# Two transformer layers on one core: the second layer's projections taken in pairs of tiles with split operands

## The reference

```python
xn = _layernorm(x, axis=-1)
x = x + attn0(xn) + ffn0(xn)      # ffn0: the two best of 8 experts for each token
xn = _layernorm(x, axis=-1)
# second attention: blocks of 64 tokens, 8 heads of 32
q = xn @ Wq + bq;  k = xn @ Wk + bk;  v = xn @ Wv + bv
probs = softmax(q @ k.T * 32 ** -0.5)          # within a block, so its rows sum to 1
attn = (probs @ v) @ Wo + bo
# second mixture: each of 8 experts takes the 512 tokens with its highest scores
scores = (xn @ Wg.T).T
x = x + attn + ffn1(xn, scores)
```

## Time and profile before

| | |
|---|---|
| median of 3 runs | 825.96 us (825.92 to 827.94) |
| the profiled execution | 833.11 us |
| its span, from the first to the last instruction | 831.3 us |
| busy share of the span | PE 93%, DVE 68%, POOL 54%, ACT 47% |
| mean granted PE clock | 0.973 of full speed |
| DMA | 114.92 MB, 138 GB/s over the span |

### The profile page before, as it was taken

How to read it: one execution, slowest core, us unless ns; L and a number is a source line. 1 busy time by engine, 2 the same in 40 slices (tenths; PEclk the granted TensorE clock), 3 DMA queues, 4 the chain that set the end, 5 groups by cost and what they waited for, 6 DMA issues and landing times.

```text
span 831.3 us, 20019 instructions
## 1 busy us (share of the span) xinstructions
PE 772.4 (93%) x6524; PEld 685.8 (82%) x6524; DVE 566.8 (68%) x1351; ACT 390.2 (47%) x936; POOL 448.6 (54%) x553
## 2 busy tenths in 40 slices
PE   6989989999999999999969999989889879999993
PEld 4867754899999999999959999867678668888883
DVE  5766776566666666667557777689999665677651
ACT  5343425444444444444415554536667564455430
POOL 3756666044445443569478888313358343666335
PEclk9999999999999999999989999969999998999997
DMA  8666632233343433344266666324547754665324
GB/s 268 229 192 234 219 110 77 74 111 121 117 125 110 121 110 122 108 144 144 80 193 200 198 196 194 108 46 112 115 100 168 201 180 140 139 140 141 65 26 50
DMA packets 140606, 114.92 MB, mean 138 GB/s; under 512 B 49890, under 2 KB 130786, under 8 KB 140516
## 3 DMA queue, kind: packets, MB, share of 16 engines
q1 hardware_dynamic: 127652, 87.94, 35.2%
q0 software_dynamic: 12288, 25.31, 13.3%
q10 hardware_dynamic: 576, 0.52, 0.2%
HBM read 68.77 MB, written 40.76 MB: 132 GB/s over the span
## 4 chain that ended last, share of the span: by engine, by line
PE 75%; DVE 9%; issue 7%; another core or an unknown queue 3%; ACT 3%; POOL 1%; DMA 0%; POOLq 0%; DVEq 0%; ACTq 0%
PE bank L838 15%; PE banks L856 12%; PE bank L1066 11%; PE bank L896 8%; PE banks L1082 4%; PE banks L766 3%; PE banks L777 3%; PE banks L712 2%; PE bank L976 2%; PE bank L825 2%; PE bank L905 2%; PE banks L905 2%; PE bank L959 2%; PE banks L911 1%
## 5 line engine op out<-in xcount | busy, mean ns | idle before, releaser
L838 PE MATMUL bank<-rw,rt 128*128 128x128 f32 x1136 | 138.6, 275 | 0.9 <-ACT rw L1170 0.6
L838 PEld LDWEIGHTS bank<-rw,rt 128*128 128x128 f32 x1136 | 132.5, 192 | 1.8 <-issue 1.3
L856 PE MATMUL banks<-r_split,rt_split 128*128 x852 | 118.7, 289 | 0.1
L1994 POOL TENSOR_TENSOR rw<-r,rw 128x128 f32<-128x128 f32 x64 | 41.3, 646 | 137.1 <-DMA rw<-in_sin_q 137.1
L856 PEld LDWEIGHTS banks<-r_split,rt_split 128*128 128x128 f32 x852 | 106.0, 190 | 0.3 <-issue 0.3
L1066 PE MATMUL bank<-r_split 128*128 128x512 f32 x384 | 91.5, 398 | 4.6 <-issue 4.5
L1982 POOL DMA_INDIRECT rows_by_expert<-rw,slots x64 | 66.5, 1039 | 46.7 <-DVE slots L1500 28.8
L1066 PEld LDWEIGHTS bank<-r_split 128*128 128x128 f32 x384 | 73.3, 193 | 20.2 <-issue 5.1
L1609 DVE TENSOR_TENSOR rt_split<-rw,rt_split 128x512 fp32r<-128x512 f32 x71 | 54.1, 763 | 49.4 <-ACT rt_split L1221 49.4
L1603 DVE TENSOR_TENSOR rw<-rw 128x512 f32<-128x512 f32 x71 | 53.5, 753 | 43.3 <-ACT rw L1215 43.2
L2100 POOL DMA_INDIRECT out_x<-r,idx x32 | 50.2, 1569 | 59.9 <-DVE r L1880 52.2
(11 more groups left out here) (255 smaller groups left out, 1646.7 us busy)
## 6 DMA issues: line engine op xcount, KB each, us to landing
rt<-in_w SPq DMA_DIRECT2D x24, 512.0 KB, 4.1
rw<-rows_by_expert SPq DMA_DIRECT2D x71, 128.0 KB
results_by_slot<-rw SPq DMA_DIRECT2D x71, 128.0 KB, 2.0
r<-in_w SPq DMA_DIRECT2D x16, 512.0 KB
rw<-in_x SPq DMA_DIRECT2D x16, 256.0 KB
rw<-in_sin_q SPq DMA_DIRECT2D x32, 128.0 KB
rw<-x_layer SPq DMA_DIRECT2D x32, 128.0 KB
rows_layer<-rw SPq DMA_DIRECT2D x32, 128.0 KB
```

Source lines behind the costliest of these rows:

```text
L838: last = pe.matmul(bank[1 + t % 2][:, k * P:(k + 1) * P], c_w1[:, t % 2, c, k * P:(k + 1) * P], c_xT[:, t % 2, c, :], start=c == 0, stop=c ...
L856: last = pe.matmul(bank[6 + t % 2][:, 0:D], h[:, t % XB, c, :], w[:, ds(e2, 1), o + c * D:o + (c + 1) * D], start=n == 0, stop=n == 3 * HC ...
```

## The change

- Stage D works in units of two tiles (NU = 16). PE transposes four 128x128 blocks of a unit into one bank (`transpose_unit`), ACT writes the high part (`high_xT`), DVE the low part (`low_xT`).
- Queries and keys of a unit: 4 output blocks of 256 columns, each 6 float32r matmuls (`queries_keys`, 24 in all). Values and scores together: 264 columns for each tile, 6 matmuls each (`values_scores`, 12 in all).
- The normalised tiles are written by ACT (`normal_unit`, Identity with scale and bias, as L1135 does in stage A) instead of DVE. ACT also moves the values and the scores out of PSUM (`keep_values_scores`).
- The bias of the values isn't added to them. As the softmax rows sum to 1, it goes through Wo: PE computes bv Wo once (`bias_of_values`), and DVE adds it to bo before stage D.
- POOL in stage D only gathers, up to eight tiles ahead in eight buffers, with a wait that the gather four tiles before has landed. SP stores x without bias (`x1_complete`), and loads and stores two tiles by one DMA. In stage E `add_x` first adds the bias to the loaded x and then the result, two POOL instructions a tile instead of one.
- The weights of the projections are split once in stage C: a copy on ACT at t = 20 and a subtraction and a small copy on DVE at t = 22.
- PE's and ACT's parts of stage D are loops of the engine as before, with two and four units a turn; before they held two tiles a turn.

```diff
+            def low_xT(u):
+                dve.wait_ge(aT_sb, NT + u + 1)
+                dve.tensor_tensor(d_lo[:, u % 2, :, :], bank[u % 2][:, :].rearrange("p (c n) -> p c n", c=DC),
+                                  d_hi[:, u % 2, :, :].bitcast(F32), ALU.subtract).then_inc(xlo_d, 1)
+            for u in range(NU + 1):          # DVE
+                if u < NU:
+                    combine(u, 0)
+                    combine(u, 1)
+                    moments_unit(u)
+                    scale_unit(u)
+                if u >= 1:
+                    low_xT(u - 1)
+            def transpose_unit(v):           # PE; 4 transposes into bank[v.k % 2]
+                pe.wait_ge(xn_r, NT + 2 * (v.u + 1))
+                if v.at_least(2):
+                    pe.wait_ge(xlo_d, v.u - 1)
+            def queries_keys(v):
+                pe.wait_ge(xlo_d, v.u + 1)
+                for b in range(2):
+                    if v.at_least(1):
+                        pe.wait_ge(qk1_sb, 4 * v.u + 2 * b - 2)
+                    for j in (2 * b, 2 * b + 1):
+                        for c in range(DC):
+                            for w, x in ((wq1_hi, d_hi), (wq1_hi, d_lo), (wq1_lo, d_hi)):
+                                last = pe.matmul(bank[2 + b][:, j % 2 * D:(j % 2 + 1) * D], w[:, c, j * P:(j + 1) * P],
+                                                 x[:, v.k % 2, c, :], start=k == 0, stop=k == 3 * DC - 1)
+            with pe.Fori(2, NU // 2) as m:
+                for k in range(2):
+                    transpose_unit(Unit(m, k, 2))
+                    project_before(Unit(m, k, 2))   # queries_keys, values_scores of the unit before
+            def step_d(v, more=True):        # ACT
+                if v.at_least(1) and more is not None:
+                    high_xT(v.back(1))
+                if more:
+                    root_unit(v)
+                    normal_unit(v)
+                if v.at_least(2):
+                    keep_queries_keys(v.back(2))
+                    keep_values_scores(v.back(2))
             def gather_y(t):                 # POOL
-                if t >= XB:
-                    pool.wait_ge(x1_r, t - XB + 1)
+                if t >= 2 * DB:
+                    pool.wait_ge(x1_r, t - 2 * DB + 1)
+                if t >= 4:
+                    pool.wait_ge(dy_in[t % 4], 32 * (t // 4))
-                pool.wait_ge(x1_r, t + 1)
-                if t >= 2:
-                    pool.wait_ge(sd.xb_out[t % 2], 16 * (t // 2))
-                pool.tensor_tensor(d_xb[:, t % 2, :], d_x[:, t % XB, :], bo1_s[:, :], ALU.add).then_inc(sd.xb, 1)
             def add_x(s):                    # POOL, stage E
+                pool.wait_ge(xbl[s.par], 16 * (s.half + 1))
+                pool.tensor_tensor(e_xb[:, s.par, :], e_xb[:, s.par, :], bo1_s[:, :], ALU.add).then_inc(bo1_r, 1)
+                pool.wait_ge(bo1_r, s.t + 1)
                 pool.wait_ge(y1_sb, s.t + 1)
-                pool.wait_ge(xbl[s.par], 16 * (s.half + 1))
                 pool.tensor_tensor(e_y[:, s.t % 4, :], e_y[:, s.t % 4, :], e_xb[:, s.par, :], ALU.add).then_inc(fin_r, 1)
```

More of the change, by code:

```diff
@@ L668, in _ @@
         def _(pe):
-            def transpose_x(z, s, xn, n=NT):
-                pe.wait_ge(z.xn, z.first + s.t + 1)
-                if s.at_least(1):
-                    pe.wait_ge(z.xT, z.first + s.t)
-                for c in range(DC):
-                    last = pe.transpose(bank[0][:, c * P:(c + 1) * P], xn[:, s.par, c * P:(c + 1) * P], ident[:, :])
-                last.then_inc(z.xT_ps, 1)
             pe.wait_ge(made, 2)
@@ L914, in _, with bias_of_values @@
-            for t in range(4):
-                step_d(Step(t // 2, t % 2))
-            with pe.Fori(2, NT // 2) as m:
-                for par in range(2):
-                    step_d(Step(m, par))
-            step_d(Step(NT // 2, 0))
+            def bias_of_values():
+                pe.wait_ge(wq1_r, 3)
+                pe.wait_ge(y_sb, ST0)
+                for c in range(DC):
+                    last = pe.matmul(bank[7][:, 0:D], bv1_b[:, c, :], wo1_s[:, c, :], start=c == 0, stop=c == DC - 1)
+                last.then_inc(bo1_ps, 1)
@@ new lines, in values_scores @@
+            def values_scores(v):
+                if v.at_least(1):
+                    pe.wait_ge(bo1_ps, 2)
+                if v.at_least(2):
+                    pe.wait_ge(sc_kept, v.u - 1)
+                par = v.k % 2
+                for i in range(2):
+                    k = 0
+                    for c in range(DC):
+                        for x, w in ((d_hi, wq1_hi), (d_lo, wq1_hi), (d_hi, wq1_lo)):
+                            last = pe.matmul(bank[4 + par * 2 + i][:, 0:D + E], x[:, par, c, i * P:(i + 1) * P],
+                                             w[:, c, 2 * D:3 * D + E], start=k == 0, stop=k == 3 * DC - 1)
+                            k += 1
+                last.then_inc(vs_ps, 1)
@@ new lines, in root_unit, with normal_unit @@
+            def root_unit(v):
+                act.wait_ge(mom_r, NT + 2 * (v.u + 1))
+                if v.at_least(2):
+                    act.wait_ge(rs_r, NT + v.u - 1)
+                act.activation(d_sd[:, v.k % 2, :], d_mv[:, v.k % 2, :, 1], ACT.Sqrt, bias=eps_c[:, :]).then_inc(std_r, 1)
+            def normal_unit(v):
+                act.wait_ge(nm_r, NPR + v.u + 1)
+                if v.at_least(2):
+                    act.wait_ge(xn1_out[v.k % 2], 16 * v.pair)
+                    act.wait_ge(aT_ps, NT + v.u - 1)
+                for i in range(2):
+                    act.activation(d_xn[:, v.k % 2, i, :], d_x[:, v.k, i, :], ACT.Identity,
+                                   bias=d_nm[:, v.k % 2, i:i + 1], scale=d_rs[:, v.k % 2, i:i + 1]).then_inc(xn_r, 1)
@@ new lines, in step_d @@
+            def step_d(v, more=True):
[4 more added lines that the diff above has]
+                    normal_unit(v)
+                if v.at_least(2):
+                    keep_queries_keys(v.back(2))
+                    keep_values_scores(v.back(2))
+            for k in range(DB):
+                step_d(Unit(0, k, DB))
+            with act.Fori(1, NU // DB) as m:
+                for k in range(DB):
+                    step_d(Unit(m, k, DB))
```

303 lines of the change are left out of this document (144 added, 159 removed).

## The result

The changed kernel takes 850.41 us (median), 1.030 times the kernel before on the same chip (interval 1.026 to 1.034): 24.5 us slower, where 7.6 us less were forecast and 835.7 was the worst case named. Two later comparisons, on other chips, gave 1.029 and 1.031. The profiled execution took 851.61 us, with a span of 849.9.

What follows compares the result with a forecast made beforehand. PE was taken to bound stage D before the change, POOL's gathers after it. Stage D's gain of 15.9 us, less 0.3 in stage C and 8.0 in stage E, gave 7.6 us less: 818.4 us, range 809 to 828.

Steps and rivals of the forecast that it cites:

- Stage D, POOL: Stage D: four gathers a unit make POOL the bound at 5.3 us, above PE's 4.87; stage gain 15.9 us.
- the three values for the pitch: Stage D, time from gather to gather on POOL: 1.37 us taken, ends 1.32 (never meeting DVE's additions) and 1.50 (always).
- PE, DVE, ACT: Stage D, work per two-tile unit: PE 4.87 us, DVE 4.8, ACT 4.8 to 4.9, none exceeding POOL.
- The ends: Stage D's end: last gather done 504.1, landed 508.0, then 14.15 us of work; stage E starts at 522.2.
- Stage C: Stage C, splitting the weights once on ACT and DVE: costs 0.3 us, bounds 0 and 2.
- Bias of the values: Before stage D, four PE instructions (0.9 us) and one DVE addition: hidden behind DVE's wait for the first gather, otherwise 1.3 us.
- Stage E: Stage E, POOL's second addition a tile: costs 8.0 us (search 1, threshold and ranks 1.8, one-hots 5.2), bounds 2 and 18.
- E swallowed nothing: Rival: stage E hides POOL's new addition under DVE's PSUM work, costing 2 us; kernel at 812.4 us; chance 0.20.
- Exclusion on gathers: Rival: DVE and POOL exclude each other, gather pitch 1.50, stage E costs 17.2; 9.7 us slower, 835.7; chance 0.13.
- The loop through four engines: Rival: stage D's dependency loop through DVE, ACT and PE takes 6.0 us a unit; 825.8 us, no change; chance 0.12.
- gathers that wait for `x1_r`: Stage D, named sign that the forecast is wrong: POOL's gathers wait for the combination of tiles.
- a unit over 5.8 us: Stage D, named sign that the forecast is wrong; a two-tile unit was expected at 5.3 to 5.7 us.

Runs made afterwards that it cites:

- e1: Changed kernel plus one 128x512 memset on POOL behind each tile's two gathers in stage D: 830.34 us, ratio 1.0047 to the kernel before.
- e3: Changed kernel with gathers of the first four tiles only, the other 28 reusing their rows (results differ): 806.14 us, ratio 0.978 to the kernel before.
- e7: Changed kernel plus a 128x16 memset on POOL behind each tile's two gathers, on the chip without stalls: 808.44 us, ratio 0.9991 to the kernel before.
- e16: Changed kernel with POOL's bias addition back in stage D, gathers three tiles ahead, one addition a tile in stage E: 835.95 us, ratio 1.0057.
- e5: Kernel before without POOL's bias addition in stage D (results differ), on the chip without stalls: 814.48 us, ratio 1.0070 to the kernel before.
- e18: Changed kernel unaltered, run again on the fifth chip: 858.57 us, ratio 1.0305 to the kernel before.
- e10: Kernel before, unaltered, run again on the third chip: 827.29 us, ratio 1.0001.
- e9: Changed kernel unaltered, run again on the third chip: 850.39 us, ratio 1.0293 to the kernel before.

## Where the prediction held and where it failed

- **Stage D, POOL: this step failed.** "A unit has 4 gathers ... 5.3 us a unit, more than PE's 4.87. POOL becomes the bound." The step gave a gather a price on POOL alone. I looked for what others do to a gather (DVE holding it, the DMA share going to 0.80) and never for what gathers do to others. POOL's addition stood in the sum as a cost that goes away; it was also the break that kept PE running. Its price for that was nothing, without a reason given. What the runs show in its place is a wait of 32.9 us at one copy of ACT alone, and a stage D that is 17.4 us longer instead of 15.9 shorter; with breaks (e1) or without most gathers (e3) the wait is gone.
- Its small terms: the pitch of bare gathers is (457.64 - 416.75) / 31 = 1.32 us, and their mean went from 1052 ns to 1010. The prediction's own working gives 0.09 us for meetings with DVE and then takes 0.05; neither is there, and of the three values for the pitch the lowest was right.
- **PE, DVE, ACT:** 4.72 to 4.76 us a unit against 4.87; the biased copy took 0.465 us against "at most 4 x 0.4", 0.26 us a unit more, and the unit came out as said all the same. Held.
- **The ends:** without stalls e7 needs 105.5 us to stage E's first row maximum. Its mean pitch is the 1.37 that I took, but by luck: it comes from the memset behind every second gather. The forecast's 522.2 lies 105.5 behind its first gather too, though for the stage's start, some 2.2 us earlier than that maximum. Held within 2.2 us.
- **Stage C:** first gather at 416.75 in both traces, and 414.80 against 414.23 on the third chip; 0.3 was said. Held. **Bias of the values** through PE: no trace of it on the path. Held.
- **Stage E:** 6.9 us against 8.0. One-hots 4.6 against 5.2; all before them 2.1 (within the scatter) against 2.8; the end 0.1. Held, and e16 ties it to the cause named. The rule beside it (the Trainium skill, SBUF — State Buffer, "Who interferes with whom"), that a VectorE instruction with two SBUF inputs contends with a GpSimd instruction that reads SBUF, agrees with the one-hots' 4.6 us for eight more additions.
- **Rivals.** E swallowed nothing. Exclusion on gathers: not there, 1010 ns. The loop through four engines: e3 has a unit at 4.72 us, not 6.0. None of them was it. Two of the signs named as wrong came true, gathers that wait for `x1_r` (22.1 us) and a unit over 5.8 us (PE's units 0 to 15 start 7.75 us apart on average, at 433.98 to 550.26), and they were signs of something that no rival held. A third, PE or ACT without idle time, didn't: they stood idle too much.
- **The sum of both:** where nothing stalls, -17 in D and +7 in E should have been about -10 us, and e7 measured 0.9991 (0.9961 to 1.0020). Some 9 us are missing. Stage F in e7 was 6.8 us longer than e5's, by PE's wait for rows and the lower clock behind it, which the prediction had no term for. The rest may be that the kernel before is quicker in D and E on that chip than on those where I have its trace; that stays open. So even without stalls "faster" at 0.77 was too sure.

## What to carry to other kernels

An instruction that looks like a cost on an engine may be the pause that another engine lives on. Before a change packs indirect DMAs closer on POOL, look at the stretches of the present trace where they already run bare, and read what PE's and ACT's rows say there; a wait for PE put down to "remote" while PE's work is long recorded as done is the sign. And before a version is judged by such an effect, run it against the old one on more than one chip.

## What the runs showed of the hardware

- Indirect DMAs issued by POOL 1.30 us apart hold up TensorE's work, or its signals, for 0.5 to 15 us at a time (15.4 in e18), on four of the five chips above and in the first traces. ACT and DVE stand still behind it, though their own instructions keep their lengths (464 ns for the copy in the changed kernel, 465 in e1). With a break of 0.81 us after every second gather (3.1 us a tile) it is gone; with 0.60 us (2.9), or 0.81 after every fourth (2.86), it isn't. Whether break or rate decides is open.
- It isn't bandwidth: in the 12 us of the second stall the DMA share is 0.30, at 87 GB/s, and the kernel before runs stage D at 0.65 and 189 GB/s. The Trainium skill (SBUF — State Buffer, "Who interferes with whom") says that DMA never contends with a compute engine. Here compute engines stand still while gathers are issued, up to 15 us at a time. Whether the transfers do that or their issuing on POOL isn't shown, so the sentence of the page is neither confirmed nor refuted. Whether PE's matmuls are late or only their signals can't be told from these records, whose ends are modelled.
- One of the five chips shows none of it. There the kernel before is 16 us faster than in the first comparison, and the kernels run there are 9 to 14 us ahead at stage A's last scatter. It may be that scatters in long runs cost the kernel before as much on the others; breaks there were not tried.
- A POOL addition with two operands in SBUF, put beside a DVE that is busy throughout, cost 4.6 us in eight tiles (28.2 to 32.8 in e10 and e9); moved back to stage D it is gone (28.7 in e16).
- A wait of 5.07 us on PE for gathered rows (e7) goes with 10.2 us at a granted clock of 0.50, which begin within it, and the stage was 6.8 us longer than with a wait of 0.17 (e5).
